# An attention and mixture-of-experts block on one core: PSUM rings of three single banks for scores and exponents become two pairs and two banks, and the values are multiplied once

## What is computed

```
h      = layernorm(x)                                   # 16 x 512 x 128
Q,K,V  = h @ W_q + b_q, h @ W_k + b_k, h @ W_v + b_v    # 16 heads of 8 features
scores = (Q K^T + Q . rel_k[clip(k - q, -2, 2) + 2]) / sqrt(8), causal
attn   = softmax(scores)
out    = attn @ V + sum_k attn[q, k] * rel_v[clip(k - q, -2, 2) + 2]
x      = x + layernorm(out @ W_o + b_o)
x      = x + layernorm(shared_and_routed_experts(layernorm(x)))
```

## Time and profile before

| | |
|---|---|
| median of 3 runs | 1068.61 us (1067.13 to 1070.38) |
| the profiled execution's own time | 1068.33 us |
| its span, first to last instruction | 1066.6 us |
| TensorE matmul busy over the span | 927.1 us (87%) |
| VectorE busy | 851.5 us (80%) |
| GpSimd busy | 727.4 us (68%) |
| ScalarE busy | 677.7 us (64%) |
| mean granted TensorE clock | 0.944 of full speed |

### The profile page before, as it was taken

One profiled execution on the slowest core, in us unless ns is written; L12 is line 12 of the kernel. 1 busy time (PEld: TensorE's weight loads), 2 busy tenths in 40 slices (PEclk: granted clock), 3 DMA queues, 4 the chain that ended last, 5 costly groups with the idle time before them and its releaser, 6 DMA issues. The chain is left out here.

```text
span 1066.6 us, 23874 instructions
## 1 busy us (share of the span) xinstructions
PE 927.1 (87%) x7783; PEld 538.8 (51%) x7783; DVE 851.5 (80%) x2060; ACT 677.7 (64%) x1303; POOL 727.4 (68%) x939
## 2 busy tenths in 40 slices
PE   2769889999899899998998999987378999999995
PEld 0324445444445454444454544433156777777774
DVE  5668788888988888889888888985368878778784
ACT  2127677677676776776767767665146676676773
POOL 4145586775866768758668677465347898898986
PEclk8669999999999999999999999988689999999998
DMA  2610010100100101001001010002324555545441
GB/s 50 162 38 19 27 42 21 42 32 22 48 22 35 39 22 43 31 22 50 20 35 41 21 43 32 21 11 65 107 69 126 172 148 164 160 142 172 156 150 30
DMA packets 61446, 70.77 MB, mean 66 GB/s; under 512 B 9504, under 2 KB 39072, under 8 KB 61344
## 3 DMA queue, kind: packets, MB, share of 16 engines
q1 hardware_dynamic: 58976, 68.99, 20.5%
q10 hardware_dynamic: 2368, 0.48, 0.3%
HBM read 43.75 MB, written 8.65 MB: 49 GB/s over the span
## 5 line engine op out<-in xcount | busy, mean ns | idle before, releaser
L1102 DVE TENSOR_REDUCE mx<-ps_s 128x1 f32<-128x512 f32 (+2 forms) x640 | 408.1, 683 | 76.8 <-PE ps_s L1505 74.3
L781 ACT ACTIVATE prob<-ps_e 128x512 f32<-128x512 f32 x640 | 349.1, 599 | 130.2 <-PE ps_e L1461 130.1
L623 POOL TENSOR_SCALAR_AFFINE_SELECT prob<-prob 128x516 f32<-128x516 f32 (+1 forms) x320 | 172.8, 565 | 185.7 <-ACT prob L781 185.7
L1484 PE MATMUL ps_s<-ks,qs 63*128 63x512 f16 (+3 forms) x1024 | 217.9, 312 | 25.7 <-DVE mx L1102 11.9
L1461 PE MATMUL ps_e<-qs,ks 64*128 64x512 f16 (+3 forms) x1024 | 195.8, 307 | 16.4 <-DMA qs<-mT 8.5
L724 POOL TENSOR_TENSOR hidden_low<-hidden,hidden_high 128x512 fp32r<-128x512 f32 x144 | 191.0, 1354 | 21.2 <-ACT hidden_high L970 19.9
L1521 PE MATMUL ps_av<-prob,vp 128*32 128x512 f32 (+3 forms) x2048 | 181.8, 451 | 14.6 <-POOL prob L623 14.4
L970 ACT CAST hidden_high<-hidden 128x512 fp32r<-128x512 f32 x160 | 98.0, 613 | 34.5 <-DVE hidden L1409 28.9
L1461 PEld LDWEIGHTS ps_e<-qs,ks 64*128 64x128 f16 x1024 | 60.0, 95 | 114.0 <-ACT prob L781 65.6
L1484 PEld LDWEIGHTS ps_s<-ks,qs 63*128 63x128 f16 x1024 | 64.8, 95 | 88.9 <-DVE mx L1102 63.2
L1505 PE MATMUL ps_s<-masked_at,below_r 64*128 64x128 bf16 (+3 forms) x640 | 109.4, 212 | 0.0
(11 more groups left out here) (174 smaller groups left out, 1800.1 us busy)
## 6 DMA issues: line engine op xcount, KB each, us to landing
gate_rows<-gates_dram SPq DMA_DIRECT2D x128, 256.0 KB, 3.6
qs<-qh SPq DMA_DIRECT2D x128, 32.0 KB
qs<-ql SPq DMA_DIRECT2D x128, 32.0 KB
xnT_dram<-oT SPq DMA_DIRECT2D x16, 256.0 KB, 2.0
xeT<-xnT_dram SPq DMA_DIRECT2D x16, 256.0 KB, 2.8
out<-result SPq DMA_DIRECT2D x16, 256.0 KB, 2.3
ks<-kh SPq DMA_DIRECT2D x124, 32.0 KB
ks<-kl SPq DMA_DIRECT2D x124, 32.0 KB
```

The lines of the kernel that those rows point to most:

```text
L623: pool.affine_select(out=v, in_=v, compare_op=ALU.is_ge, fill=0.0, base=-2, pattern=cols, channel_multiplier=-1).then_inc(S["p_masked"], 1)
L781: act.activation(prob[g % 2][:, u, b, :], ps_e[bank][:, :], ACT.Exp, scale=SCALE).then_inc(S["e_done"], 1)
L1102: dve.tensor_reduce(out, src, AX.X, ALU.max).then_inc(s_free[bank], 1)
L1484: pe.matmul(scores[:, at:at + P * (qt + 1)], qs[par][rows, 2 * g + off, P * qt:P * qt + P], ks[par][rows, 2 * g + off, 0:P * (qt + 1)], st ...
```

## The change

- **Scores' ring.** Instead of three single banks it has two tensors of two banks (`ps_s` is 2 x 512 columns). Both score units of a round go to one pair, the semaphore `s_full` is raised once, and one maximum instruction reads 1024 columns for two heads. `S_RING` counts a pair as one use; a pair is waited for when the first unit of its round is issued.
- **Exponents' ring.** It has two banks in place of three; its order of uses is the same.
- **Values.** Before, `v1` multiplied the tokens shifted by one (keys at distance 1) and `v0` those in place. Now only `v0` is multiplied; VectorE adds the two differences to it, into `v_back` and `v_near[:, 0]`, and two DMAs on SyncE's queue move `v_back` down by one token into `v_near[:, 1]` (`shift_values`).
- **Small VectorE instructions.** The larger of the two near scores is taken once for all heads (`s_best`), and one instruction with it replaces three in `max_half`; the score rows are scaled by 1/16 when ScalarE copies them, and the exponential of the near scores is scaled back by 16. The reciprocal and the product of `av_tok_out` run once for two groups of heads (g odd) in place of once for each.

```diff
-AT = {"e_sums": 1, "av2": 2, "v1": 3, "v0": 5, "m1": 5, "av3": 6, "xT": 6, "s_tok": 7, "oT": 8, "q": 9,
+AT = {"e_sums": 1, "av2": 2, "v0": 5, "m1": 5, "av3": 6, "xT": 6, "s_tok": 7, "oT": 8, "q": 9,
       "av0": 10, "oproj": 10, "k": 10, "m0": 15, "av1": 17, "xn2": 18, "logits": 19}
...
-def ring_order(uses, units):
-
-    return [what for _, what in sorted([(2 * AT[w] - 0.5, w) for w in uses] + [(i, f"{units}{i}") for i in range(NUNIT)])]
-
-
-S_RING = ring_order(("v0", "v1", "oproj"), "s")
-E_RING = ring_order(("xT", "oT", "q", "k"), "e")
-RING = 3
+def ring_order(uses, units, each):
+
+    return [what for _, what in sorted([(2 * AT[w] - 0.5, w) for w in uses] +
+                                       [(each * i, f"{units}{i}") for i in range(NUNIT // each)])]
+
+
+S_RING = ring_order(("v0", "oproj"), "s", 2)
+E_RING = ring_order(("xT", "oT", "q", "k"), "e", 1)
+RING = 2
...
-        ps_s = [ctx.enter_context(nc.psum_tensor(f"ps_s{i}", [P, SEQ], F32)) for i in range(RING)]
+        ps_s = [ctx.enter_context(nc.psum_tensor(f"ps_s{i}", [P, 2, SEQ], F32)) for i in range(RING)]
...
+            def shift_values(st):
+
+                wait_apart(sp, S["back_made"], st.at(st.a + 1, 1), passed["sp"])
+                need(sp, S["near_ready"], st.at(4 * st.a, 4))
+                sp.dma_start(v_near[1:P, 1], v_back[0:P - 1]).then_inc(S["v_shifted"], 16)
+                sp.dma_start(v_near[0:1, 1, 1:NT], v_back[P - 1:P, 0:NT - 1]).then_inc(S["v_shifted"], 16)
...
-            def values_out(st, i):
-                n, bank = st.s_use(f"v{i}")
+            def values_out(st):
+                n, bank = st.s_use("v0")
+                v = ps_s[bank][:, 0].rearrange("p (t c) -> p t c", t=NT)
 
                 dve.wait_ge(S["s_full"], n + 1)
+                dve.wait_ge(S["v_ready"], st.at(st.a + 1, 1))
+                need(dve, S["v_shifted"], st.at(32 * st.a, 32))
+                dve.tensor_tensor(v_back[:, :, :], v, dv[:, 0, :].unsqueeze(1).to_broadcast([P, NT, P]),
+                                  ALU.add).then_inc(S["back_made"], 1)
                 need(dve, S["near_ready"], st.at(4 * st.a, 4))
-                if i == 0:
-
-                    dve.wait_ge(S["v_ready"], st.at(st.a + 1, 1))
-                dve.tensor_tensor(v_near[:, i], ps_s[bank][:, :].rearrange("p (t c) -> p t c", t=NT),
-                                  dv[:, 1 - i, :].unsqueeze(1).to_broadcast([P, NT, P]),
+                dve.tensor_tensor(v_near[:, 0], v, dv[:, 1, :].unsqueeze(1).to_broadcast([P, NT, P]),
                                   ALU.add).then_inc(s_free[bank], 1)
 
-            def s_max(st, i):
-                g, u, b = i // (2 * NU), i % (2 * NU) // 2, 1 - i % 2
-                n, bank = st.s_use(f"s{i}")
-                scores, (off, qt, _) = ps_s[bank][:, :], S_UNITS[u][0]
-                h = 2 * (2 * g + off) + b
+            def s_max(st, r):
+                g, u = r // NU, r % NU
+                n, bank = st.s_use(f"s{r}")
+                scores, (off, qt, _) = ps_s[bank][:, :, :], S_UNITS[u][0]
+                h = 2 * (2 * g + off)
                 if len(S_UNITS[u]) == 1:
-                    out, src = mx[:, QT0 + qt, h:h + 1], scores
+                    out, src = mx[:, QT0 + qt, h:h + 2], scores
                 elif u == 2:
-                    out, src = mx[:, QT0 + qt, h:h + 3:2], scores.rearrange("p (n c) -> p n c", n=2)
+                    out = mx[:, QT0 + qt, h:h + 4].rearrange("p (n b) -> p b n", b=2)
+                    src = scores.rearrange("p b (n c) -> p b n c", n=2)
                 else:
-                    out, src = mx[:, 0:QT0 + 1:4, h], scores.rearrange("p (n c) -> p n c", n=NT)
+                    out = mx[:, 0:QT0 + 1:4, h:h + 2].rearrange("p r b -> p b r")
+                    src = scores.rearrange("p b (n c) -> p b n c", n=NT)
 
                 dve.wait_ge(S["s_full"], n + 1)
                 dve.tensor_reduce(out, src, AX.X, ALU.max).then_inc(s_free[bank], 1)
...
+                own.mark(dve.tensor_tensor(s_best[:, :, :], s_tok[:, 0], s_tok[:, 1], ALU.max))
...
-                own.mark(dve.tensor_tensor(mxa[:, :, hs], mx[:, QT0:, hs], s_tok[:, 0, :, hs], ALU.max))
-                own.settle()
-                own.mark(dve.tensor_tensor(mx[:, QT0:, hs], mxa[:, :, hs], s_tok[:, 1, :, hs], ALU.max))
-                own.settle()
-
                 need(dve, S["p_ready"], st.at(2 * (s - 1) + half + 1, 2))
-                dve.tensor_scalar(m16[:, :, hs], mx[:, QT0:, hs], 1.0 / M_UNIT, None, ALU.mult).then_inc(S["m16_ready"], 1)
+                dve.scalar_tensor_tensor(m16[:, :, hs], mx[:, QT0:, hs], 1.0 / M_UNIT, s_best[:, :, hs],
+                                         ALU.mult, ALU.max).then_inc(S["m16_ready"], 1)
                 dve.wait_ge(S["m16_ready"], st.at(2 * s + half + 1, 2))
                 for k in range(2):
-                    last = dve.scalar_tensor_tensor(d01[:, k, :, hs], m16[:, :, hs], -M_UNIT, s_tok[:, k, :, hs],
-                                                    ALU.mult, ALU.add)
+                    last = dve.tensor_tensor(d01[:, k, :, hs], s_tok[:, k, :, hs], m16[:, :, hs], ALU.subtract)
...
-                need(dve, S["o_ready"], st.at(NGRP * s + g, NGRP))
+                if g % 2 == 0:
+                    need(dve, S["o_ready"], st.at(2 * s + g // 2, 2))
                 v = ps_misc[:, :].rearrange("p (t j c) -> p t j c", t=NT, j=4)
-                par = s % 2
-                own.mark(dve.tensor_tensor(den[:, :, :], v[:, :, :, D], p_near[par][:, :, 4 * g:4 * g + 4], ALU.add))
+                par, hs = s % 2, slice(4 * (g % 2), 4 * (g % 2) + 4)
+                own.mark(dve.tensor_tensor(den[:, :, hs], v[:, :, :, D], p_near[par][:, :, 4 * g:4 * g + 4], ALU.add))
                 cols = slice(4 * g * D, 4 * g * D + 4 * D)
-                dve.tensor_tensor(num[:, :, :, :], v[:, :, :, 0:D], near[par][:, :, cols].rearrange(
+                dve.tensor_tensor(num[:, :, hs, :], v[:, :, :, 0:D], near[par][:, :, cols].rearrange(
                     "p t (j d) -> p t j d", d=D), ALU.add).then_inc(S["misc_free"], 1)
+                if g % 2 == 0:
+                    return
                 own.settle()
                 own.mark(dve.reciprocal(rden[:, :, :], den[:, :, :]))
                 own.settle()
 
                 dve.wait_ge(S["misc_free"], st.misc(f"av{g}") + 1)
-                dve.tensor_tensor(o_tok[:, :, cols].rearrange("p t (j d) -> p t j d", d=D), num[:, :, :, :],
-                                  rden[:, :, :].unsqueeze(3).to_broadcast([P, NT, 4, D]),
+                both = slice(4 * (g - 1) * D, 4 * (g + 1) * D)
+                dve.tensor_tensor(o_tok[:, :, both].rearrange("p t (j d) -> p t j d", d=D), num[:, :, :, :],
+                                  rden[:, :, :].unsqueeze(3).to_broadcast([P, NT, 8, D]),
                                   ALU.mult).then_inc(S["o_ready"], 1)
...
-                            s_max(st, i)
+                            if i % 2:
+                                s_max(st, i // 2)
...
+                if i % 2 == 0:
+                    pair = s_bank(st, f"s{i // 2}")
+                s_part(st, i, pair[:, 1 - i % 2], 0)
+                return pair
...
-            def values(st, n):
-                u = s_bank(st, f"v{n}")
+            def values(st):
+                u = s_bank(st, "v0")[:, 0]
                 for i in range(NT):
-                    last = pe.matmul(u[:, i * P:i * P + P], xnT[:, 1 - n + i * P:1 - n + i * P + P], wv[:, :],
+                    last = pe.matmul(u[:, i * P:i * P + P], xnT[:, 1 + i * P:1 + i * P + P], wv[:, :],
                                      start=True, stop=True)
```

More of the change, by code:

```diff
@@ L296, in block_kernel @@
         mx = sb("mx", [P, QT0 + NT, H])
-        mxa = sb("mxa", [P, NT, H])
+        s_best = sb("s_best", [P, NT, H])
         m16 = sb("m16", [P, NT, H], F16)
@@ L643, in near_half @@
                 if half == 0:
-                    for n in range(2):
-                        pool.wait_ge(s_free[st.s_use(f"v{n}")[1]], st.s_turn(f"v{n}") + 1)
-                    need(pool, S["o_ready"], st.at(NGRP * (s - 1), NGRP))
+                    pool.wait_ge(s_free[st.s_use("v0")[1]], st.s_turn("v0") + 1)
+                    pool.wait_ge(S["v_shifted"], st.at(32 * (st.a + 1), 32))
+                    need(pool, S["o_ready"], st.at(2 * (s - 1), 2))
                 hs = slice(half * 8, half * 8 + 8)
@@ L827, in v_out @@
                 act.copy(vp[st.a % 2][:, :, :, 0:D].rearrange("p t h d -> p (t h) d"),
-                         ps_s[bank][:, :].rearrange("p (c d) -> p c d", d=D)).then_inc(S["v_ready"], 1)
+                         ps_s[bank][:, 0].rearrange("p (c d) -> p c d", d=D)).then_inc(S["v_ready"], 1)
             def oT_out(st):
@@ L840, in s_rows_out @@
                 act.wait_ge(S["misc_full"], st.misc("e_sums") + 1)
-                act.copy(s_rows[:, :], ps_misc[0:64, :]).then_inc(S["misc_free"], 1)
```

(24 more changed lines are left out.)

40 lines of the change are left out of this document (19 added, 21 removed).

## The result

The changed kernel takes 1131.8 us (median of 4, 1124.0 to 1136.8), the one before 1069.0 us: 1.058 times as long, 95% interval 1.050 to 1.066. It is slower, as forecast, but by 63 us where 24 were forecast, outside the range. The profiled execution is the longest of the four, 1136.8 us; the mean granted clock of the four is 0.895, 0.928, 0.895 and 0.913. A ratio is estimated from the runs and need not be the quotient of the two medians; it leaves out the one run that is over 1.5% above the fastest of its own kernel, 1171.0 us in experiment 1.

What follows compares the result with a forecast made beforehand. Waits on buffers, no engine full, were taken as the bound: longer exponents' waits less vanished scores' waits and one value product gave +1.65 us per step, +24.8 us over fifteen, so 1068.3 becomes 1093 us; range 1060 to 1114 us.

Steps and rivals of the forecast that it cites:

- e17: Second exponent unit of round 8: with two banks it waits for ScalarE's oT copy, 0.5 us.
- e19: Second exponent unit of round 9: with two banks it waits for the second instruction of `q_out`, 1.25 us.
- rival C: TensorE's clock drops in half to all steps, 10 to 21 us on top: 1103 to 1114 us; chance 0.13.
- both rings (6.35 + 0.5 - 0.5 - 3.6): Per step: eight exponent-unit waits 6.35 us, smaller places 0.5, less GpSimd's lateness 0.5 and scores' waits 3.6.
- The term for GpSimd (-0.5): Before 321.64 us TensorE waits 0.91 us for normalised rows; a later TensorE finds about half gone, -0.5 us.
- A: Deeper scores' ring wins if ScalarE's queue terms come under about 1.2 us per step: 1051 us; chance 0.20.
- e1: Second exponent unit of round 0: with two banks it waits for the exponential of e39, 1.0 us.
- e23: Second exponent unit of round 11: with two banks it waits for an earlier unit's exponential on ScalarE, 1.1 us.
- e31: Second exponent unit of round 15: with two banks it waits for an earlier unit's exponential on ScalarE, 0.7 us.
- e39: Exponent unit whose exponential stands behind `av_out` and the logits on ScalarE; e1 waits for it, 1.0 us.
- B: No change: TensorE's waits for GpSimd absorb 1.2 us more, step within 0.2 us: 1065 to 1072 us; chance 0.11.
- D: `maxima_out` lands later behind 16 DMAs on SyncE's queue, keys about 1.7 us later; counted within the high bound.

Runs made afterwards that it cites:

- experiment 1: The kernel before with only the exponents' ring cut from three banks to two: 1163.9 us, 1.093 times as long.
- experiment 3: The changed kernel with both rings put back to three single banks, one maximum per score unit, the removed work kept out: 1051.6 us, 0.985.
- experiment 4: The changed kernel with first exponent units of eight rounds issued again into the same bank, 16 more units per step: 1103.9 us, 1.035.
- experiments 4 to 6: experiment 4, then its kernel with repeats only in rounds 1, 9, 10 and 11 (1115.2 us), and only in 15, 16, 18 and 0 (1105.8 us).
- experiment 2: The kernel before with both rings changed, both value products and all small VectorE instructions kept: 1138.4 us, 1.069.
- experiments 3 and 8: experiment 3, and the kernel before with only the single value product and the shift by DMA, rings of three: 1063.2 us, 0.995.

## Why the prediction was right and wrong

**The direction and the mechanism** were right and are shown: experiment 1 makes the whole loss with the exponents' ring alone, and the units wait where and for what the prediction said. By the starts above, e17 lost 0.52 us (0.5 forecast) and e19 another 1.26 (1.25 forecast).

**The failed step is the clock, which the sum puts at nothing.** The sum adds waits and work at a granted clock of 1.00, and a lower clock is only rival C: "if half to all steps drop so", at 1.4 us each from the earlier trace rows, with a chance of 0.13. The runs showed a clock of 0.89 in twelve of thirteen steps and a price of 3.2 us a step (47.9 against 44.7). Thirteen steps of 44.7 us are 581 us: of the 67.8 us that the full steps of the profiled execution grew, 27 are the order and 41 the clock; in the two runs with a mean clock of 0.913 and 0.928 the clock's part must be smaller. Without it, 15 times 2.25 us on 1068.3 us would make 1102 us, an estimate that lies within the range. The prediction's own sign, a clock under 0.9 in the full steps, came.

C had the direction, and both its chance and its price were too low. Its price was that of another case: the drop keeps the clock down for about 10.5 us a step now, and in the step of the earlier trace rows (0.92 of 44.16 us) it was about 7 us. The share of TensorE's busy time, from which C argues (86%), does not decide it: in experiment 1 steps that TensorE filled to 83% (39.01 of 46.78 us) had 1.00, and other steps of the same kernel 0.87. Nor does the stretch from 683 us: the like of it has 0.85 in experiment 3, whose steps are at 1.00 but for one. The Trainium skill (TensorE: Matmul & The Clock Gate, "What's actually happening") puts activity as what releases the throttle; experiment 4 agrees, as repeated matmuls took 28 us off.

**The step length at full clock** was nearly right, and in part by luck: "+1.65 us" on 42.75 makes 44.4, and experiments 4 to 6 show 44.7. But the usual step is 42.45, so the change is +2.25 us; the rings cost 0.9 us more than forecast, and the longer step that the sum starts from and the removed work make up for most of it:

| term, us per step | forecast | measured at full clock |
|---|---|---|
| both rings (6.35 + 0.5 - 0.5 - 3.6) | +2.75 | +3.65 (experiment 2: 46.10 - 42.45) |
| of it the exponents' ring, put in first | | +4.33 (experiment 1) |
| of it the scores' pairs, put in behind it | | -0.68 (experiment 2 against 1) |
| one value product and small instructions | -1.1 | -1.40 (44.7 against 46.10) |
| sum | +1.65 | +2.25 |

"I take all 3.6 us as gone" is right of the waits, which did go. But 3.6 us was read in a trace with three exponents' banks. In experiment 1 the new exponents' waits had taken 2.4 us of that place already, so that the pairs brought only 0.68 us. For the same reason the 4.33 us can't be set against the 6.35: they are what was left when those waits had gone. Which of the ring terms the missing 0.9 us belong to stays open. The term for GpSimd (-0.5) is not the one: TensorE's own waits for it fell by more, from 22.7 to 6.6 us between 130 and 680 us, about 1.2 us per step. The value product, "all on its path", was worth 0.12 us by itself with three banks.

**Rivals.** A needed the queues on ScalarE under 1.2 us per step; they stayed, and e1, e23 and e31 waited (e1, at 348.98 us, 0.39 us for the exponential of e39). B is refuted by the step length. D did not matter: TensorE waited for the transfer of the maxima once between 94 and 740 us, for 1.2 us. The cost of nothing for the two shift DMAs fits experiments 3 and 8: faster with them. The merged maximum, VectorE's busy time and the vanished waits for maxima came as forecast.

## What to carry to other kernels

Take a wait's worth from the trace only for one change at a time. When two rings feed one engine that works in order, making one shallower uses up part of the waits at the other, and deepening that other one then gives back only what is left (0.68 us of 3.6 here). A ring must be deep enough to cover the instructions that stand between two of its reads, not only the reads: count the copies of the reading engine that sit in it. And where a change makes TensorE wait more, and some steps of the same trace already show a lowered clock, price that clock in every step as part of the likeliest case; here it was the larger part of the loss. Then keep the parts of a change apart: here the removed work alone, with the old rings, is the fastest version (1051.6 us).

## What the runs showed of the hardware that was not expected

Issuing 16 exponent units more beside the 40 of each step, in places where TensorE waited, shortened a kernel by 28 us. The clock was 0.50 for about 10 us of nearly each 47.9 us step, in those steps always behind round 18, though TensorE had waited more in rounds 9 to 11. Repeats in either of two places of the step raised it, those in rounds 15, 16, 18 and 0 more than those in rounds 1 and 9 to 11 (nine of thirteen steps at 1.00 with the late ones, three of thirteen with the early ones, none without). Steps of one kernel with the same work (experiment 1) had 1.00, 0.96, 0.93, 0.90 and 0.87 in one execution, and took 46.78, 47.89, 48.82, 50.29 and 51.54 us, one of each. What decides in which steps it falls, and how far, stays open.
